# Second layer's modulation products of a two-layer transformer: from the linear attention to the places around the layer norm behind it

## What is computed

```python
mod = (_silu(L1_c) @ L1_wmod).reshape(L1_c.shape[0], 6, 1, -1)   # the products that the change moves
sa, ca, ga, sb, cb, gb = (mod[:, 0], mod[:, 1], mod[:, 2], mod[:, 3], mod[:, 4], mod[:, 5])
...
h = _layernorm(x, axis=-1) * (1 + ca) + sa
x = x + ga * attention(h)
h = _layernorm(x, axis=-1) * (1 + cb) + sb
x = x + gb * ffn(h)
...
# attention of the first layer, per chunk of 64 tokens:
S = S + jnp.einsum('bhtd,bhte->bhde', ki, vi)
Z = Z + ki.sum(axis=2)
num = jnp.einsum('bhtd,bhde->bhte', qi, S)
den = jnp.einsum('bhtd,bhd->bht', qi, Z)[..., None] + 1e-06
```

## Time and profile before

| | |
|---|---|
| median of 3 runs | 708.69 us (708.49 to 711.36) |
| the profiled execution | 708.0 us, its span from first to last instruction 706.1 us |
| mean granted TensorE clock | 0.988 |
| PE busy | 654.3 us (93%) |
| DVE busy | 457.2 us (65%) |
| ACT busy | 334.4 us (47%) |
| POOL busy | 149.7 us (21%) |

### The profile page before, as it was taken

How to read it: one execution, slowest core, us unless ns; L and a number is a source line. 1 busy time by engine, 2 the same in 40 slices (tenths; PEclk the granted TensorE clock), 3 DMA queues, 4 the chain that set the end, 5 groups by cost and what they waited for, 6 DMA issues and landing times.

```text
span 706.1 us, 10697 instructions
## 1 busy us (share of the span) xinstructions
PE 654.3 (93%) x3990; PEld 405.8 (57%) x3990; DVE 457.2 (65%) x970; ACT 334.4 (47%) x531; POOL 149.7 (21%) x194
## 2 busy tenths in 40 slices
PE   4999979999999879899999998897999999999996
PEld 3667647777777656455444434483554444368884
DVE  5668787777777388778888602557788886242223
ACT  5334243333333423345567684561564657843332
POOL 3002224555555601310000000031100001003331
PEclk9999799999999999999999999999999999999999
DMA  7602410000000002663000000037410000050001
GB/s 263 227 0 91 128 44 0 24 23 22 1 0 1 0 1 75 190 186 92 2 2 2 1 2 1 1 125 227 137 54 2 2 2 2 20 160 1 1 0 59
DMA packets 36415, 38.34 MB, mean 54 GB/s; under 512 B 4034, under 2 KB 35292, under 8 KB 36108
## 3 DMA queue, kind: packets, MB, share of 16 engines
q1 hardware_dynamic: 36364, 37.67, 17.0%
HBM read 30.11 MB, written 7.34 MB: 53 GB/s over the span
## 4 chain that ended last, share of the span: by engine, by line
PE 47%; issue 22%; POOL 12%; DVE 11%; ACT 3%; DMA 2%; SPq 2%; POOLq 0%; DVEq 0%; ACTq 0%
POOL it_lo L1602 9%; PE psum L782 9%; PE psum L742 8%; PE psum L768 8%; PE psum L454 4%; DVE m L1285 3%; PE psum L455 3%; PE psum L456 3%; POOL wd L1581 2%; PE psum L771 2%; PE psum L745 2%; PE psum L471 2%; PE psum L570 1%; DVE mx L1285 1%; SPq L345 1%
## 5 line engine op out<-in xcount | busy, mean ns | idle before, releaser
L962 ACT ACTIVATE pt<-psum 128x1024 f32<-128x1024 f32 (+1 forms) x192 | 148.1, 811 | 93.2 <-PE psum L771 65.1
L1285 DVE TENSOR_REDUCE mx<-psum 128x1 f32<-128x512 f32 (+3 forms) x216 | 132.4, 665 | 16.3 <-PE psum L742 8.3
L742 PE MATMUL psum<-kr,qr 96*128 96x512 bf16 (+3 forms) x384 | 108.6, 332 | 5.7 <-DVE m L1285 2.7
L768 PE MATMUL psum<-qr,kr 99*128 99x512 bf16 (+3 forms) x384 | 97.6, 327 | 1.5 <-ACT pt L962 1.3
L1602 POOL TENSOR_TENSOR it_lo<-it,it_hi 128x512 fp32r<-128x512 f32 x48 | 67.3, 1402 | 146.2 <-ACT it_hi L1006 144.6
L782 PE MATMUL psum<-pt,vp 128*32 128x512 f32 (+3 forms) x768 | 81.7, 498 | 0.0
L454 PE MATMUL psum<-h_hi,wf_hi 128*128 128x512 f32 x192 | 75.4, 393 | 1.7 <-issue 1.7
L742 PEld LDWEIGHTS psum<-kr,qr 96*128 96x128 bf16 x384 | 36.3, 98 | 68.0 <-DVE mx L1285 29.4
L1006 ACT CAST it_hi<-it 128x512 fp32r<-128x512 f32 x48 | 29.9, 623 | 95.7 <-DVE it L1360 95.7
L455 PE MATMUL psum<-h_lo,wf_hi 128*128 128x512 f32 x192 | 74.8, 390 | 0.0
L456 PE MATMUL psum<-h_hi,wf_lo 128*128 128x512 f32 x192 | 74.8, 389 | 0.0
(11 more groups left out here) (201 smaller groups left out, 1087.1 us busy)
## 6 DMA issues: line engine op xcount, KB each, us to landing
qr<-parts_scratch SPq DMA_DIRECT2D x48, 128.0 KB, 2.7
kr<-parts_scratch SPq DMA_DIRECT2D x48, 128.0 KB, 2.6
parts_scratch<-parts SPq DMA_DIRECT2D x12, 384.0 KB, 3.2
wmod<-in_L_wmod SPq DMA_DIRECT2D x1, 1536.0 KB, 6.3
parts_scratch<-qr SPq DMA_DIRECT2D x4, 384.0 KB, 3.2
x<-in_L_attn_x SPq DMA_DIRECT2D x2, 512.0 KB, 4.3
wmod<-in_L_wmod SPq DMA_DIRECT2D x1, 1024.0 KB, 5.3
packed<-in_L_ffn_gate_W_packed SPq DMA_DIRECT2D x1, 1024.0 KB, 7.2
```

The source lines that it names most:

```text
L742: m = pe.matmul(b, qr[0:PARTS_ROWS, c, h, (qt - 4 * c) * P:(qt - 4 * c + 1) * P], kr[0:PARTS_ROWS, ch, h, 0:w], start=True, stop=not diag)
L768: m = pe.matmul(bank[4 + 2 * at[0] + j][:, 0:w], kr[0:PARTS_ROWS + 3, kt // 4, h, (kt % 4) * P:(kt % 4 + 1) * P], qr[0:PARTS_ROWS + 3, c, ...
L962: act.activation(pt[:, n % 4, :, 0:w], psum[:, b:b + 2, 0:w], ACT.Exp, scale=0.25).then_inc(S["ex"], 1)
L1285: dve.tensor_reduce(dst, bank[at[0]][:, 0:k * w].rearrange("p (k w) -> p k w", k=k), AX, ALU.max).then_inc(S["p1_mx"], 1)
```

## The change

PE makes three fill products a tile (`idle(3, 7)`) in tiles 1 to 7 of the linear attention, where two modulation products a tile were in tiles 2 to 7. Eight modulation products, each behind one fill product, stand behind `update(0)` in place of 20 fill products, and four behind `layer_norm(1)` in place of 8. They go to bank 5, the copy on DVE stands behind the halves of the layer norm, and the MLP on PE waits for it. `wmod1` lies over `raw0` and a part of `vp`, no longer over `scale`; it is loaded as soon as the first layer's weights have been split. POOL's fill of `vp` is cut in four and stands behind `it_lo` of units 4 to 7.

```diff
-        (wmod0, raw0), (wmod1,), (scale,), (parts, vp), (b_hi, m_hi) = overlay(
+        (wmod0, raw0), (_, wmod1), (scale,), (parts, vp), (b_hi, m_hi) = overlay(
...
-            [("wmod1", [P, KC, 1536], F32)],
+            [("wmod0_", [P, KC, 1536], F32), ("wmod1", [P, KC, 1536], F32)],
...
-            sp.wait_ge(S["mod_mm"], 2)
+            sp.wait_ge(S["wt_hi"], 5)
+            sp.wait_ge(S["wt_lo"], 4)
             load(wmod1[:, :, :], a["L1_wmod"].rearrange("(c p) n -> p c n", p=P), "ld_wmod1")
...
-            sp.wait_ge(S["mod_mm"], 3)
+            sp.wait_ge(S["mod_mm"], 2)
             for j in range(FC[0] // 2):
...
             for t in range(NT):
-                if t >= 2:
-
-                    if t == 2:
-                        pe.wait_ge(S["ld_wmod1"], 16)
-                    modulation(wmod1, 1, 7, 2 * t - 4)
-                    m = modulation(wmod1, 1, 7, 2 * t - 3)
-                    if t == 7:
-                        m.then_inc(S["mod_mm"], 1)
+                if t >= 1:
+                    idle(3, 7)
...
             pe.wait_ge(S["q_e"], 8)
-            pe.wait_ge(S["mod_cp"], 3)
             attention_transposes(0)
...
-            idle(20, 4)
+            pe.wait_ge(S["ld_wmod1"], 16)
+            for j in range(8):
+                idle(1, 4)
+                modulation(wmod1, 1, 5, j)
             layer_norm(1)
-            idle(8, 4)
+            for j in range(8, 12):
+                idle(1, 4)
+                m = modulation(wmod1, 1, 5, j)
+            m.then_inc(S["mod_mm"], 1)
             pe.wait_ge(S["ln_f"], 8)
             pe.wait_ge(S["ln_hl"], 8)
+            pe.wait_ge(S["mod_cp"], 3)
             mlp(0)
...
-                        act.wait_ge(S["vp_ones"], 1)
+                        act.wait_ge(S["vp_ones"], 4)
...
             normalise(7)
-            modulation_copy(2, 1, 7, 0, 12)
             modulation_rest(0)
...
             halves(1)
+            modulation_copy(2, 1, 5, 0, 12)
             modulation_rest(1)
...
                     scaled(1)
 
-                    pool.wait_ge(S["mod_mm"], 3)
-                    pool.wait_ge(S["wt_hi"], 5)
-                    pool.wait_ge(S["wt_lo"], 4)
-                    pool.memset(vp[:, :, :, :], 1.0).then_inc(S["vp_ones"], 1)
...
                     if n % 2 == 1 and f == 0 and n // 2 + 2 < FC[f]:
                         scaled(n // 2 + 2)
+                    if f == 0 and 4 <= n < 8:
+                        if n == 4:
+                            pool.wait_ge(S["mod_mm"], 3)
+                        pool.memset(vp[:, 2 * n - 8:2 * n - 6, :, :], 1.0).then_inc(S["vp_ones"], 1)
+                        pool.wait_ge(S["vp_ones"], n - 3)
```

## The result

The changed kernel takes **715.68 us**, median of five runs (713.65 to 718.53), against 708.69 us before, now also five runs (708.49 to 711.36): ratio 1.0077, 95% interval 1.005 to 1.0104, slower. The profiled execution took 715.7 us, its span is 713.6 us; before it was 708.0 and 706.1. There are 7.5 us of span to find. The kernel before was timed again beside each group of experiments; its medians there were 710.35 (e1 to e4), 710.99 (e5 to e8), 710.24 (e9 to e11) and 711.38 us (e12), so the experiments compare by their ratios and not by their times.

A forecast was written before the change was run, and what follows sets the result against it. DVE narrowly bounds the linear attention, DVE and the scales the update, a POOL-ACT-DVE loop the MLP. -0.65 + 0.15 + 2.5 + 2.0 = +4.0 on 708.0 gives 712.0, median 0.7 above: 712.7 us; range 706.5 to 715.5, own 711 to 715.5.

The forecast's parts named there:

- the early fall: PE's clock falls before the layer norm's end: four pairs at double, 2.7 us, and 2.3 in the MLP; 716 us.
- the first rival: The forecast itself: clock falls ahead of the MLP and the `vp` fills cost; about 712.7 us, chance 0.40.
- Linear attention and scales, -0.65: Linear attention to DVE's update: last low weight half, scales and update each come 0.65 us earlier.
- PE's 3 us at the attention's end are lost: Update transposes and projection end about 3 us earlier on PE; 2.4 us of that lost waiting for DVE.
- The rival that it reaches the end if the scales land earlier: Attention's end: scales landing before about 80.7 us let PE's 3 us gain through; 705.8 us, chance 0.12.
- Copy, +0.15: DVE's copy of the modulation columns now stands between the layer norm's halves and the MLP: +0.15 us.
- Split fill, +2.5: First MLP: quarter fills of `vp` delay `it_lo`, holding up two `wf_lo` by about 1.05 us each; +2.5, bounds 0 to 4.
- The 0.2 us for each fill that meets the bit operations: First MLP: fills behind units 4 and 6 meet DVE taking bits apart; 0 to 0.9 us each, taken as 0.2.
- fills hidden: First MLP: `wf_lo` goes ahead of the delayed `it_lo`, so DVE's loop runs on; 708.2 or 710.2 us, chance 0.20.
- Clock ahead of the MLP, +2.0: 1.2 GHz shortly before the MLP: last pairs cost 0.3 us, first MLP unit 1.7; +2.0, bounds 0 to 5.
- The bound of 5: Upper bound of the clock's cost ahead of the MLP: four pairs at double, 2.7 us, and 2.3 in the MLP.
- the cover that I gave the eight pairs, 0.6 us: Behind the update: eight fill-and-modulation pairs end about 95.5 us, before the layer norm's input at 96.16; 0.6 us spare.

The follow-up runs named there:

- e1: Changed kernel with the fill of `vp` in one piece again, ahead of POOL's MLP work: 713.97 us, ratio 1.0034.
- e4: Kernel before with only the fill of `vp` cut in four behind `it_lo` of units 4 to 7: 713.77 us, ratio 1.0057.
- e5: Changed kernel, one-piece `vp` fill, moved products bare in blocks of eight and four, followed by 10 and 4 fill products: 719.82 us, ratio 1.0132.
- e8: Kernel before with the change's place for `wmod1` and the scales loaded ahead of the `raw` loads: 710.83 us, ratio 1.0001.
- e9: Kernel before with 12 fill products instead of 28 around the layer norm, modulation products left in the linear attention: 711.55 us, ratio 1.0018.
- e11: Changed kernel, one-piece `vp` fill, two fill products per moved product, first four scale blocks loaded ahead of the `raw` weights: 707.15 us, ratio 0.9969.
- e12: Like e11, but with the one-piece `vp` fill behind POOL's whole work of the first MLP: 708.68 us, ratio 0.9958.
- e3: Changed kernel with the first four scale blocks loaded ahead of the four `raw` weights: 712.71 us, ratio 1.0016.
- e10: Changed kernel, one-piece `vp` fill, two fill products instead of one ahead of each moved modulation product: 710.42 us, ratio 1.0.
- e6: Changed kernel, one-piece `vp` fill, six bare moved products in PE's `update(0)` wait, six behind it, then 13 and 8 fill products: 714.02 us, ratio 1.0035.
- e2: Changed kernel with 12 fill products in PE's 2.9 us wait for DVE in `update(0)`: 714.38 us, ratio 1.0055.
- e7: Changed kernel with one-piece `vp` fill and without the fill products in the linear attention: 715.31 us, ratio 1.0055.

## Why the prediction was right, and where its terms were off

The forecast was 712.7 us, with its own range 711 to 715.5 inside the wide one of 706.5 to 715.5. The median, 715.68, is just above both and 3.0 above the forecast; the early fall that the first rival puts at 716 is what happened. The measured 0.77% is slower by the limit of 712.2 that the prediction set itself, a case to which it gave 0.41, less than the 0.49 for "same". The signs and the mechanisms were those forecast; the profiled execution lies 3.7 above the 712.0 of the sum, of which the clock's term makes about 2.1, the linear attention 0.3, the fill -0.5, and what the sum left out some 1.5. The terms of the sum of +4.0 came out so:

- **Linear attention and scales, -0.65.** Measured -0.34. The clock held, and DVE's waits fell from 1.2 + 0.9 to 0.5 + 0.2 us. Counted from the first key-value product, the last normalised output came 1.17 us earlier, but the last low weight half, on which SP and the scales hang, only 0.38. Of the 1.5 us of waiting that vanished, 0.8 lay behind that half. Of the 0.7 ahead of it a part came back in DVE's own work: `cum` of 73.94 took 0.72 us while POOL's `xn` of 73.64 ran, where in the kernel before the one of 73.51 began behind POOL's and took 0.44.
- **PE's 3 us at the attention's end are lost.** Right: transposes at 76.84 and 78.74, the projection's end 2.7 us earlier from the first key-value product on, and then 2.89 us in which PE waits for DVE. The rival that it reaches the end if the scales land earlier is refuted by e3: the next thing in line is DVE's own block 0, POOL, block 1, and 1.5 us is all that early scales bring.
- **Copy, +0.15.** Right: 0.16 us at 105.84, in front of the MLP.
- **Split fill, +2.5.** Measured +2.0, shown twice, by taking it away (e1) and by adding it alone (e4). The two `wf_lo` grew by 1.02 us each, as worked out (1.05). The 0.2 us for each fill that meets the bit operations was nothing: the one of 141.42, which met the end of the fill of 140.61, took 0.30 us for 0.28. The rival "fills hidden" was 0.1 us away and didn't occur: `wf_lo` starts 0.11 us after `it_lo`. The fill of 130.88 ran beside the `wf_lo` of 130.77 and lengthened neither (0.96 and 0.98 us); the displaced `it_lo` of 139.39 did. By the rule on the port pair that I set beside it (the Trainium skill, page "SBUF — State Buffer", section "SBUF: two separate sides") it is the reading that counts, and these rows agree.
- **Clock ahead of the MLP, +2.0.** This is the term that was mis-sized: +4.1 (2.78 + 1.45, less the copy), 2.6 of it ahead of the MLP, where I had 0.3, and 1.45 in the MLP, where I had 1.7. The step that failed in it is where the fall begins. I expected it shortly before the MLP, with one or two of the last pairs in it. It came at 92 us, with the second pair, lasted through the sixteen transposes (3.34 us) and came back for 3.4 us at the MLP's start (0.63 us a product for 0.39). The first eight pairs, six of which took 1.1 us instead of 0.58, were no longer hidden: they ended at 99.62, 2.1 us behind the layer norm's input. The bound of 5 covers the sum, but not for its reason: it put the last four pairs at double, and those ran at full rate (0.58 us each, from 102.80 on) and cost nothing. I had also put the early fall outside the likeliest case. What makes the clock fall here is shown in part. Fewer fills bring it without the moved products (e9), and twice the fills hold it beside them (e10, e11 and e12), so too few long products is the reading that fits best. But in e9 and e10 the pauses changed along with the fills, in e6 the clock fell in a block of bare moved products without a pause and with 21 fills in all, and in e8 it fell with all 28. Amount, order and pauses were not separated. Of the cover that I gave the eight pairs, 0.6 us, nothing was to spare once a pair had two fills: in e10 the transposes came at 99.02, 0.3 us late, which with the copy is the 0.43 us that e10 to e12 keep over before.
- Not in the sum: 1.1 us at the kernel's start and 0.4 in the second layer's second attention, neither from the change as far as the traces show.

## What to carry over

Fill products that "nobody reads" may be load-bearing: before they are traded for useful short work, count what runs behind them at half rate if the clock falls. In these traces the fall cost 0.5 us with 12 fills alone, 4.1 with the useful work in it, and did not come ahead of the MLP in the three kernels with 24 fills. A cheap operation put into a slot of an idle engine can still stop another engine: look at what starts within its span, not only at who waits for its result. And a gain on one engine is worth only the distance to the next chain: here 2.7 us on PE became 0.3 us, and 1.8 once the scales came first.

## What the runs showed of the hardware

- POOL's fill of `vp` (a memset, 3.51 us, which reads nothing) held up DVE's single-input fp32 operations from SBUF to SBUF for as long as it ran: a cast of 0.42 us took 3.38 (e5), three operations of 0.17 took 3.08, 3.01 and 2.95 (e11), eight `xn` 5.55 for 2.9 (e6). It held up neither additions of PSUM and SBUF nor statistics (e12). The section of the Trainium skill named above says that the lock concerns VectorE's two-port modes against any GpSimd operation, and two-input ones only against a reading one. The two-input rows agree (`wf_lo` of 130.77, 0.98 us beside the fill and 2.00 beside `it_lo`); the single-input ones do if they ran in such a mode, which no row shows.
- In the nine kernels with three fills a tile in the linear attention, the clock there held in five (after, e1, e3, e5, e11) and fell at 74, 76, 77 and 78 us in e2, e12, e10 and e6, whose code up to there hardly differs. With the old products it fell at 71, 71, 76 and 75 us (before, e4, e8, e9). Without either it fell at 76 us (e7). So the fills may make a fall rarer and don't exclude it, and one trace tells little of where it lies in the next execution.
- At the kernel's start the first products of 512 fp32 columns took 0.47 and then 0.39 us in the execution of before, and 0.76 and then 0.63 in that of after, until 20.3 us. These are the durations of the same products at 2.4 GHz and at 1.2 GHz later in the trace (0.63 at 106.82), so PE ran at the lower level there, although the profile prints 1.00 for that stretch. The three traces that start at 0.47 and stay at the full rate (before, e2, e5) have their first key-value product at 54.9 to 55.1 us, the other eleven at 56.2 to 58.3. With the code there the same, the bias product of the first tile starts at 20.32 in after and 19.31 before, and this 1.0 us is nearly all of the 1.1 ahead of the first key-value product. Why the level differs from one execution to the next is open.
- The scale of such effects is that of the change: single runs of the kernel before lie between 707.3 and 718.0 us.
